# Eight-core layer on Trainium2: the third tile's statistics planned one projection earlier, and the halves of one PSUM tile used in turn

## The reference

```python
xn = layernorm(x)
qkv = xn @ Wqkv + bqkv;  q, k, v = split(qkv, 3)
q = q / norm(q);  k = k / norm(k)
kv = sum_over_tokens(k * v)                     # 1 x 1024 per batch
attn = (q * kv) @ Wout + bout
h = silu(xn @ w1.T * s1) * (xn @ w2.T * s2)     # 1024 -> 4096
h = gelu(h @ h1.T * sh1);  h = gelu(h @ h2.T * sh2)   # 4096 -> 4096, twice
out = x + attn + h @ w3.T * s3
```

## Time and profile before

| | |
|---|---|
| median of 3 runs (range) | 3054.74 us (3052.47 to 3118.59) |
| the profiled execution, its own time | 3049.96 us |
| its span on the slowest core (core 1) | 3048.1 us |
| spans of the 8 cores | 3030.1 to 3048.1 us |
| mean granted TensorE clock of the cores | 0.971 to 0.981 |
| TensorE matmul busy | 2870.9 us, 94% of the span |
| VectorE, ScalarE, GpSimd busy | 378.7, 464.8, 219.8 us |
| HBM read over the span | 486.66 MB |

### The profile page before, as it was taken

The page is one execution under the profiler, slowest core; times in us unless marked ns, Lnnn a source line. Parts: engine busy times, 40 slices in busy tenths (PEclk is TensorE's granted clock), DMA queues, the critical chain, the costliest instruction groups (busy, mean ns, idle before and its releaser), DMA issues.

```text
span 3048.1 us, 30724 instructions; the slowest of 8 cores (3030.1 to 3048.1 us)
## 1 busy us (share of the span) xinstructions
PE 2870.9 (94%) x13056; PEld 1281.3 (42%) x13056; DVE 378.7 (12%) x440; ACT 464.8 (15%) x463; POOL 219.8 (7%) x420
## 2 busy tenths in 40 slices
PE   3876899899999999999988899999999999999998
PEld 0323344344444444444433344444444444444443
DVE  3255211432000000000011221100000000000011
ACT  1443211450000000000020031100000000000100
POOL 0000000110000000000000000000000000000000
PEclk9988999999999999999999999999999999999999
DMA  6545344884444444444445644444444444444453
GB/s 162 130 120 122 85 81 73 160 141 90 76 76 76 76 76 76 76 76 76 76 104 119 146 88 72 81 76 76 76 76 76 76 76 76 76 76 76 76 118 90
DMA packets 76598, 278.93 MB, mean 92 GB/s; under 512 B 8752, under 2 KB 8880, under 8 KB 76464
## 3 DMA queue, kind: packets, MB, share of 16 engines
q0 software_dynamic: 59904, 218.13, 42.6%
q1 hardware_dynamic: 16560, 58.85, 6.3%
HBM read 486.66 MB, written 8.39 MB: 162 GB/s over the span
## 4 chain that ended last, share of the span: by engine, by line
PE 83%; DMA 5%; DVE 2%; ACT 1%; issue 0%; SPq 0%; DVEq 0%; ACTq 0%
PE PD L198 23%; PE PC L198 23%; PE PB L198 19%; PE PA L198 18%; DMA xs<-x_fm 4%; DMA out_fm<-os 1%; DVE os L699 1%; DVE os L693 0%; ACT os L665 0%; DVE tmp_f L259 0%; DVE xb L210 0%; ACT Ab L624 0%; ACT sq L214 0%; DVE Ab L498 0%; DVE Gb L261 0%
## 5 line engine op out<-in xcount | busy, mean ns | idle before, releaser
L198 PE MATMUL PC<-Gb,wr 128*128 128x512 bf16 x2080 | 478.2, 382 | 31.0 <-DVE Gb L261 31.0
L198 PE MATMUL PD<-Gb,wr 128*128 128x512 bf16 x2080 | 476.3, 382 | 0.0
L198 PE MATMUL PB<-Gb,wr 128*128 128x512 bf16 x1728 | 392.1, 380 | 4.1 <-DVE rstd_b L242 4.1
L198 PE MATMUL PD<-Ab,wr 128*128 128x512 bf16 x1536 | 354.4, 385 | 27.6 <-ACT os L665 27.6
L198 PE MATMUL PC<-Ab,wr 128*128 128x512 bf16 x1536 | 347.2, 379 | 0.9 <-ACT os L665 0.9
L198 PE MATMUL PA<-Gb,wr 128*128 128x512 bf16 x1536 | 347.2, 379 | 0.0
L198 PEld LDWEIGHTS PC<-Gb,wr 128*128 128x128 bf16 x2080 | 203.6, 98 | 284.2 <-issue 42.8
L198 PEld LDWEIGHTS PD<-Gb,wr 128*128 128x128 bf16 x2080 | 204.9, 99 | 249.7 <-issue 8.0
L198 PEld LDWEIGHTS PB<-Gb,wr 128*128 128x128 bf16 x1728 | 169.4, 98 | 209.4 <-issue 6.5
L191 POOL DMA_DIRECT2D wr<-h_t x256 | 135.1, 528 | 1616.6 <-PE PB L198 798.4
L198 PEld LDWEIGHTS PD<-Ab,wr 128*128 128x128 bf16 x1536 | 151.7, 99 | 215.6 <-issue 40.1
(11 more groups left out here) (83 smaller groups left out, 1001.5 us busy)
## 6 DMA issues: line engine op xcount, KB each, us to landing
wr<-h_t POOLq DMA_DIRECT2D x256, 512.0 KB, 5.9
xs<-x_fm SPq DMA_DIRECT2D x96, 512.0 KB, 5.1
wr<-w_t POOLq DMA_DIRECT2D x96, 512.0 KB, 6.0
wr<-wqkv_t POOLq DMA_DIRECT2D x56, 512.0 KB, 7.0
out_fm<-os SPq DMA_DIRECT2D x16, 512.0 KB, 3.6
wr<-wout_t POOLq DMA_DIRECT2D x8, 512.0 KB, 6.7
cst<-consts SPq DMA_DIRECT2D x1, 64.0 KB, 1.8
ones_sb<-ones_bf SPq DMA_DIRECT2D x1, 32.0 KB, 2.9
```

Of the source, the lines that this page charges most:

```text
L198: e.matmul(p[:, h * 512:(h + 1) * 512], l, r, start=a, stop=b),
```

## The change

Two edits.

1. stats(2) with xn(2) is no longer planned between the Ln/Exp of K(1) and Q. It is planned in the round t = 0, behind V(0) and the four weight loads of K(1), and ahead of kv(0). Nothing in it is altered: 16 loads of x, 8 casts, 8 squares, 32 matmuls, the chain of six, 16 operations of normalizing.
2. In the four segments, the sum of squares goes into the first half of PA for s = 0 and 2 and into the second half for s = 1 and 3. Each half has its own record of when it is free, and the Ln reads the half of its segment. After the segments PA counts as free when both halves are.

The number of instructions on every engine stays the same, and so does the order of the weight loads on GpSimd's queue and the order of x loads on SP's queue.

```diff
@@ -428,8 +428,6 @@
                 if t == 0:
                     plan_stats(1, "PA", "PB")
-                else:
-                    plan_stats(2, "PA", "PB")
                 if t == NT1 - 1:
                     plan_qproj(4)
                 plan_proj([(wqkv[8 + i, :, :], [2 * i, 2 * i + 1]) for i in range(4)],
@@ -439,6 +437,8 @@
                                if t + 1 < NT1 else None)
                 if t == NT1 - 1:
                     st["pre_ffn"] = [dma_w(w1[0, :, :]), dma_w(w2[0, :, :])]
+                if t == 0:
+                    plan_stats(2, "PA", "PB")
                 plan_kv(kbuf, vbuf, t_rk, kev, vev)
@@ -512,6 +512,7 @@
                     seg_free = {q: [psum_free[q[0]]] for q in slots}
+                    seg_pa_free = {0: psum_free["PA"], 1: psum_free["PA"]}
                     seg_tm = [{}, {}]
@@ -561,10 +562,10 @@
-                                        def snmm(oc_=oc, jq_=jq, qslot_=qslot, tq_=tq):
-                                            t_n = mm("PA", 0, ones_sb[:, :], qslot_[:, 0:512],
+                                        def snmm(oc_=oc, jq_=jq, qslot_=qslot, tq_=tq, h_=s % 2):
+                                            t_n = mm("PA", h_, ones_sb[:, :], qslot_[:, 0:512],
                                                      start=(oc_ == 0), stop=(oc_ == DC - 1),
-                                                     waits=[tq_, psum_free["PA"]], inc="s_pe")
+                                                     waits=[tq_, seg_pa_free[h_]], inc="s_pe")
@@ -572,9 +573,9 @@
                         t_ln2 = S.op("scalar", lambda e, r=r0_: e.activation(
-                            rstdn_b[:, r:r + 512], PS["PA"][:, 0:512], AF.Ln),
+                            rstdn_b[:, r:r + 512], PS["PA"][:, r:r + 512], AF.Ln),
                             waits=[norm_last2[0], prev_rstd_kv[s % 2]], inc="s_ac")
-                        psum_free["PA"] = t_ln2
+                        seg_pa_free[s % 2] = t_ln2
@@ -594,6 +595,7 @@
                         st["kv_prev_dve"] = st["kv_done"]
+                    psum_free["PA"] = [seg_pa_free[0], seg_pa_free[1]]
                     qkvt_toks = plan_q_scale(t_rq)
```

## The result

The change made the kernel about one per cent slower: the ratio to the kernel before is 1.0099, 95% interval 1.0067 to 1.0132, that is +20 to +40 us, with +30.2 us in the middle (0.0099 x 3054.74). The forecast was +25.6 us with a range of +9 to +47.

The account below looks back on a forecast made before the run. TensorE's matmuls, busy 2870.9 of 3048.1 us, were taken to bound the kernel. +36.0 - 10.0 - 20.2 - 1.7 + 19.8 + 1.7 = +25.6 us on the median 3054.74 gave 3080.3, range 3064 to 3102.

Parts of the forecast that it names:

- first cast of stats(2): VectorE, after xn(1): the cast takes the place where kv(0) began, at 164.4 us.
- K(1) starts: TensorE behind stats(2): K(1) starts at 188.2 us, 36.0 us after V(0), with only stats(2)'s own matmuls between.
- kv(0) starts: VectorE, first block: kv(0) comes after xn(2), at 225.0 us instead of 164.37, and ends at 248.7.
- TensorE's wait at L317: In Q, TensorE idles 19.8 us for ScalarE's first square of q, held behind the Ln that waits for kv(0).
- first eviction of V(1): First block: the sum of the terms puts V(1) +25.6 us later, its start at 277.4 instead of 251.8.
- The pace of the loads: stats(2) between V(0) and K(1): two buffers in turn set 2.98 us per chunk, as in the earlier trace.
- Rival A: Crowded loads: x loads of stats(2) and xn(2) land at the segments' pace; half gives about +41, 3096, all 3111; chance 0.11.
- upper end of +56.3: Bound for slow x loads of stats(2) and xn(2): four chunks in 24.02 us, 6.0 each, give +56.3 us.
- rival D: Statistics hide in K(1)'s wait for xn(1): K(1) starts at 164.4, V(1) at 246.1, 5.7 earlier, 3049; chance 0.02.
- Edit 2 at nothing: Segments: the halves of PA cost and gain nothing; bounds zero and the whole 12.58 us wait of segment 1.
- The lower bound: If x landed at once, stats(2) takes its 11.78 us of matmuls, K(1) starts at 177.0, loss still +6.9 us.
- Rival C: Output stages: a shift of phases removes TensorE's 27.6 us wait for evictions into `os`, 3052.7, or 14.0 of it, 3066; chance 0.05.

Follow-up runs that it names:

- e1: Edit 1 alone (statistics of tile 2 behind V(0)), segments as before, against the kernel before: ratio 1.0099 [1.0066, 1.0132].
- e2: Edit 2 alone (halves of PA in turn), statistics where they were, against the kernel before: ratio 0.9997 [0.9973, 1.0020].
- e3: The changed kernel with kv(0) on VectorE between stats(2) and xn(2) instead of behind xn(2): ratio to the kernel before 1.0016 [0.9984, 1.0047].
- e9: The changed kernel once more, unaltered, for a profile: 3088.6 and 3088.7 us, a quotient of 1.009 to the kernel before, without an interval.
- e10: The kernel before with a third output buffer (rstdn_b) in the output stages: ratio 0.9864 [0.9840, 0.9889].
- e4: The kernel before with k and v of the segments in two places in turn, PA as before: ratio 0.9978 [0.9947, 1.0009].
- e5: The changed kernel with four x buffers instead of two in the first block: ratio to the kernel before 0.9998 [0.9966, 1.0030].
- e6: Built on e4, statistics of tiles 2 and 3 made in one-chunk steps between outputs of the first feed-forward stage: 2996 to 3004 us in three executions.

## Why the prediction was right

**The direction and the mechanism.** It named two holes, and both are there: the statistics between V(0) and K(1), and the wait of ScalarE's Ln for kv(0). e1 and e2 put the loss on edit 1, e3 takes the second hole away and leaves 0.16% (interval -0.16% to +0.47%).

**Step by step**, means over the eight cores of e9 beside the forecast:

```
                              forecast     measured
first cast of stats(2)           164.4        166.7
eighth cast                      184.9        185.7
K(1) starts                      188.2        189.0
kv(0) starts                     225.0        225.1
TensorE's wait at L317            19.8         20.1
first eviction of V(1)           +25.6        +29.3   (core 1 alone: +25.1)
end                              +25.6        +30.3
```

The start of K(1) is that of the chain's first operation, L237, less the 0.39 us between the two in the earlier trace rows.

**The pace of the loads.** I took that of the earlier trace rows, 2.98 us per chunk; it was (185.7 - 166.7) / 7 = 2.71. The first cast came 2.3 us later than forecast, on core 7 because its load landed only at 163.59; the two errors nearly cancel, and that is luck. The hole itself was forecast at 36.0 us and is 33.0 on average, since V(0) ends at 156.0 on average and not at core 1's 152.2. Rival A, the pace of the segments at 6.0, did not come; the upper end of +56.3 was never near. Nor did rival D: on core 7 TensorE waits 10.68 us for the first cast of stats(2), and nothing of it is hidden behind V(0).

**The size.** The middle of the measured interval, +30.2, is 4.6 us above the sum, but the interval runs from +20 to +40 and holds +25.6: no error of the sum is shown. Nor can it be settled from the profiles. In absolute time the first eviction of V(1) was forecast at 281.2 (255.57 + 25.6) and came at 281.9 in e9 and 282.6 in e1, means of eight cores, so the terms of the change fit to about 1 us. What moves is the base. The same event has a mean of 252.6 in the profile of before, on which the table above rests, and of 253.5, 256.4 and 256.6 in e10, e2 and e4, where the first block is the old one. Against all four, mean 254.8, the change is +27.5 at V(1). Core 1 of the first profile, with 255.57, was close to that mean, so the agreement on core 1 to 0.5 us is partly chance, like the 29.3 of the table.

**Edit 2 at nothing.** Right (e2: 0.9997), for the reason given: ScalarE's own order had the Ln done before the square that the matmul needs. On core 1 before:

```profile
577.11 0.60 ACT L574 ACTIVATE rstdn_b<-PA 128x512 f32<-128x512 f32 x1
...
592.32 0.63 ACT L560 ACTIVATE sq<-Gb 128x512 bf16<-128x512 bf16 x1
```

That segment 1 waits for the products is shown by e4.

**The lower bound.** I wrote that even free loads would leave +6.9. e5 went to no loss at all (0.9998), but that is no test of it: its four buffers also hasten the statistics of tiles 0 and 1, which the bound took as given. Its stretch from V(0) to K(1), 20.1 us, is below the 24.8 of the bound (177.0 - 152.2), since there xn(1) was faster as well and VectorE began with the casts at 150.4 instead of 164.4. The bound held one thing fixed that more buffers would move. From the first cast to K(1) e5 takes 19.0 us, the bound had 12.6: its loads are faster, not free.

**Rival C.** Not borne out: the tail's waits stayed (mean 23.3 to 25.1). On the slowest core they were longer than before (44.7 us on core 7, against 27.6 on core 1). That they are worth 30 us to whoever removes them (e10) is another matter.

## What to carry to other kernels

When a block of work is moved, write out each engine's new order and ask of each piece in it who waits for it and when: here the matmuls of the statistics were moved at little cost, and their tail on VectorE, which nobody needed for 300 us, pushed ahead of a product for which two engines stood. Most of the loss was given back by ordering the pieces within the move (e3), and a gain came when the moved work lay between matmuls that run anyway (e6). Work out the terms on all cores, and take the base from more than one execution: here it moved by 4 us at V(1), as much as the sum seemed to be off. And where a row names an engine as what ended a wait, look whether a load landed just before: in e5 two rows name TensorE, and both casts had waited for a load.

## What the runs showed that I had not expected

A second pair of load buffers brought the last five loads of the statistics from 2.98 to 1.41 us per 512 KB chunk, but all eight only from 2.71 to 2.28, and filled the DMA engines at once (0.99 busy, 272 GB/s): the gain lay mostly in xn(1), which ended 7.8 us sooner behind V(0). Six waits in the output stages, 1.3 to 8.2 us each on core 1 and 23.3 us together as a mean of the cores, are worth 30 us of 3050, a quarter of it in slow matmuls behind the long ones. And the same waits differ so much from core to core (7.0 to 35.2 us within e4) and from one execution to the next that they mostly decide which core is the slowest: in the executions on record with two output buffers the cores end 17 to 60 us apart, with three 10 to 22.
